# A fused RWKV-6 and FP4 feed-forward kernel: third down product among the levels, decay exponentials and tree ahead of the rounding, W and K mixed on four row groups

## The reference

```
xn = layernorm(x)
# attention: 4 heads of 64
dxa = shift(xn) - xn;  xm = xn + dxa * miu_x
lora_h = tanh(xm @ A_lora)                        # 5 groups of 32
miu_f = lambda_f + lora_h_f @ B_lora_f            # f = w, k, v, r, g
x_f = xn + dxa * miu_f
k, v, r = x_k @ Wk.T, x_v @ Wv.T, x_r @ Wr.T;  g = silu(x_g @ Wg.T)
w = td_miu + tanh(x_w @ td_A) @ td_B
S_t = diag(exp(-exp(w_t))) S_(t-1) + k_t^T v_t;   y_t = r_t @ (S_(t-1) + u * k_t^T v_t)
att = (group_norm(y) * gamma + beta) * g @ Wo.T
# feed-forward, every operand of a product rounded to FP4 in blocks of 16
h = silu(q(xn) @ q(w_gate).T) * (q(xn) @ q(w_up).T)     # 704 hidden
out = x + att + q(h) @ q(w_down).T
```

## Time and profile before

| | us |
|---|---|
| median of 3 runs (lowest to highest) | 773.11 (772.06 to 779.34) |
| the profiled execution, its own time | 776.1 |
| span of its instructions | 774.3 |
| TensorE busy | 675.0 (87%) |
| VectorE busy | 633.1 (82%) |
| ScalarE / POOL busy | 286.8 / 335.4 |
| granted TensorE clock, mean | 0.97 |

### The profile page before, as it was taken

The page is one execution under the profiler, slowest core; times in us unless marked ns, Lnnn a source line. Parts: engine busy times, 40 slices in busy tenths (PEclk is TensorE's granted clock), DMA queues, the critical chain, the costliest instruction groups (busy, mean ns, idle before and its releaser), DMA issues.

```text
span 774.3 us, 17212 instructions
## 1 busy us (share of the span) xinstructions
PE 675.0 (87%) x6873; PEld 487.6 (63%) x6873; DVE 633.1 (82%) x1093; ACT 286.8 (37%) x500; POOL 335.4 (43%) x245
## 2 busy tenths in 40 slices
PE   1386779899999999899999999989999999999986
PEld 0143667567857677567857577567756587566764
DVE  1899877789877997799877998789888898879773
ACT  2033053532525244432525336342625335252321
POOL 2465344534472354534463254533454244622540
PEclk9869699999999999999999999999999999999999
DMA  6000000000000000000000100000000000000000
GB/s 216 36 0 27 3 2 2 1 28 3 29 0 1 29 30 1 1 27 3 29 1 1 28 3 28 1 28 2 30 0 1 28 3 29 1 0 2 30 1 27
DMA packets 13986, 13.70 MB, mean 18 GB/s; under 512 B 1889, under 2 KB 13665, under 8 KB 13921
## 3 DMA queue, kind: packets, MB, share of 16 engines
q1 hardware_dynamic: 13920, 12.73, 5.1%
HBM read 8.53 MB, written 4.19 MB: 16 GB/s over the span
## 4 chain that ended last, share of the span: by engine, by line
PE 41%; DVE 29%; issue 17%; ACT 5%; POOL 5%; SPq 2%; DMA 1%; DVEq 0%; POOLq 0%; ACTq 0%
PE ft L373 7%; PE gu L348 5%; DVE xx L989 5%; PE pair L548 4%; POOL kk L1315 4%; PE pair L440 4%; PE pair L334 3%; PE pair L489 3%; PE pair L323 3%; DVE att L1077 2%; PE pair L457 2%; DVE hv L1005 2%; PE pair L410 2%; DVE att L1075 2%; DVE hv L905 2%
## 5 line engine op out<-in xcount | busy, mean ns | idle before, releaser
L1288 POOL TENSOR_TENSOR xx<-xx,xnt 128x1024 f32<-128x1024 f32 x32 | 71.7, 2240 | 73.8 <-DVE xx L989 73.7
L373 PE MATMUL ft<-wdn,raw 128*128 128x256 f32 (+1 forms) x384 | 97.8, 397 | 3.5 <-ACT raw L730 3.5
L1297 POOL TENSOR_TENSOR raw<-hv,hsc 128x352 f32<-128x352 f32 x64 | 50.7, 792 | 112.5 <-DVE hv L907 112.5
L348 PE MATMUL gu<-wgu_hi,xqt_hi 128*128 128x352 f32 x256 | 89.9, 351 | 9.0 <-DVE hv L1005 9.0
L1315 POOL TENSOR_TENSOR kk<-kk,dt 128x512 f32<-128x512 f32 x48 | 58.9, 1227 | 86.8 <-PE pair L410 75.9
L334 PE MATMUL pair<-xx,wproj 128*128 128x512 f32 x192 | 90.4, 615 | 3.7 <-POOL xx L1288 3.0
L709 ACT ACTIVATE sg<-gu 128x352 f32<-128x352 f32 x64 | 29.7, 463 | 157.5 <-PE gu L348 157.4
L373 PEld LDWEIGHTS ft<-wdn,raw 128*128 128x128 f32 (+1 forms) x384 | 69.4, 192 | 26.2 <-issue 14.0
L348 PE MATMUL gu<-wgu_lo,xqt_hi 128*128 128x352 f32 x256 | 82.9, 324 | 0.0
L348 PE MATMUL gu<-wgu_hi,xqt_lo 128*128 128x352 f32 x256 | 82.8, 323 | 0.0
L410 PE MATMUL pair<-rr,kk 64*64 64x64 f32 (+1 forms) x2880 | 70.0, 230 | 12.3 <-DVE ee L1180 8.0
(11 more groups left out here) (145 smaller groups left out, 1347.3 us busy)
## 6 DMA issues: line engine op xcount, KB each, us to landing
xl<-in_x SPq DMA_DIRECT2D x8, 512.0 KB, 3.7
out<-raw SPq DMA_DIRECT2D x8, 512.0 KB, 2.8
raw<-in_w_gu SPq DMA_DIRECT2D x1, 1408.0 KB, 9.7
wproj<-in_w_proj SPq DMA_DIRECT2D x1, 1280.0 KB, 6.6
raw<-in_w_dn SPq DMA_DIRECT2D x1, 704.0 KB, 10.1
wblora<-in_b_lora SPq DMA_DIRECT2D x8, 32.0 KB, 1.8
walora<-in_w_lora SPq DMA_DIRECT2D x1, 160.0 KB, 3.1
wtdb<-in_td_b SPq DMA_DIRECT2D x2, 64.0 KB, 2.2
```

The costliest lines, as they stand in the source:

```text
L348: mm = pe.matmul(gu[:, part * 512:part * 512 + HI], xs[:, k, b * L:(b + 1) * L], ws[:, k, c0:c0 + HI], start=(n == 0), stop=(n == len(term ...
L373: mm = pe.matmul(dn, hxt[0:w, t, :], wdn[0:w, t, :], start=(t == 0), stop=(t == KT - 1))
L1288: pool.tensor_tensor(x3, x3, xnt0, ALU.add).then_inc(s_xx, 1)
L1297: pool.tensor_tensor(blocked(to), hidden_blocks(u), bcast(hsc[:, u % 2, 0, :], BLOCK), ALU.mult).then_inc(s_hx, 1)
```

## The change

- `MIX_AT` gives w and k a second place for their second half: tile 2 of `lh`, row groups 2 and 3. ScalarE fills it with a second tanh of 64 partitions; two further 32 KB loads fill B_lora there.
- `keep_busy` is gone. Down product 2 of the step before leaves the front and is cut in two: tiles 0 and 1 behind level 2, tiles 2 to 5 behind level 3. Its add stands in VectorE's levels, behind round 1, and goes to `ot` after the attention is added (as does the fourth); `add_attention` waits for two adds and not three.
- Level 4 comes ahead of gate/up 2; HT 3 moves behind level 5, ahead of gate/up 3; level 6 ahead of down product 3. ScalarE's `hidden` 3 moves from the front's end to between keeps 5 and 6.
- VectorE's levels: `head_stats` stands ahead of product 2; scale 2 ahead of rescale 6.
- ScalarE does the decay exponentials and the affine ahead of `head_abs`; VectorE the tree ahead of `gated`, and `head_round` behind `ffn_product` 6 (step 0 keeps its own place for it). POOL adds R's xn ahead of `head_scale`.
- The query transposes and the high copy go behind G's projection and its SiLU.
- In `finish` the output projection goes ahead of HT 3, and `add_attention` ahead of the third add.

```diff
-MIX_AT = {W_MIX: [(0, 0), (0, 0)], K_MIX: [(0, 1), (0, 1)], ...
+MIX_AT = {W_MIX: [(0, 0), (2, 2)], K_MIX: [(0, 1), (2, 3)], ...
+            for f, g in ((W_MIX, 2), (K_MIX, 3)):
+                sp.dma_start(wblora[R_LORA * g:R_LORA * (g + 1), 2, :], b_lora[f]).then_inc(s_const, 16)
...
-            def keep_busy(step, n):
-
-                pe.wait_ge(s_hxt, before(step, 4))
-                for _ in range(n):
-                    pe.matmul(ft[:, 0:N], wgu_hi[:, 0, 0:P], xqt_hi[:, 0, :], start=True, stop=True)
...
+            def down_tiles(step, b, tiles):
+                if tiles[0] == 0:
+                    pe.wait_ge(s_hxt, before(step, 4) + b + 1)
+                for t in tiles:
                     w = P if t < KT - 1 else REST
                     mm = pe.matmul(dn, hxt[0:w, t, :], wdn[0:w, t, :], start=(t == 0), stop=(t == KT - 1))
-                mm.then_inc(s_dn, 1)
+                    if t == KT - 1:
+                        mm.then_inc(s_dn, 1)
@@ TensorE, front @@
                     y_transposes(prev)
-                    down(prev, 2)
                     gate_up(prev, 6)
...
                 project(pair[1], 2, R_MIX).then_inc(s_rmm, 1)
-                head_transposes_q(step)
                 pe.wait_ge(s_mix, before(step, 5) + 5)
                 pe.wait_ge(s_xx, before(step, 5) + 5)
                 project(pair[0], 3, G_MIX).then_inc(s_gmm, 1)
+                head_transposes_q(step)
@@ TensorE, finish @@
                 down(step, 2)
+                output_projection(step)
                 hidden_transposes(step, 3)
-                output_projection(step)
                 down(step, 3)
@@ TensorE, levels @@
                 level(step, 1)
-                if tail:
-                    hidden_transposes(step - 1, 3)
                 gate_up(step, 0)
                 level(step, 2)
                 if tail:
-                    keep_busy(step, 3)
+                    down_tiles(step - 1, 2, range(0, 2))
                 gate_up(step, 1)
                 level(step, 3)
                 if tail:
-                    keep_busy(step, 3)
+                    down_tiles(step - 1, 2, range(2, KT))
+                level(step, 4)
                 gate_up(step, 2)
-                level(step, 4)
-                if tail:
-                    keep_busy(step, 3)
+                level(step, 5)
+                if tail:
+                    hidden_transposes(step - 1, 3)
                 gate_up(step, 3)
-                level(step, 5)
+                level(step, 6)
                 if tail:
                     down(step - 1, 3)
-                level(step, 6)
@@ ScalarE, front @@
-                act.activation(lh[:], both(pair[0][:]), ACT.Tanh).then_inc(s_lh, 1)
+                act.activation(lh[:, 0:2], both(pair[0][:]), ACT.Tanh).then_inc(act_own, act_did.one())
+                act.activation(lh[HS:P, 2], pair[0][0:HS, 0:N], ACT.Tanh).then_inc(s_lh, 1)
...
-                head_abs(step)
                 act.wait_ge(s_wmm, through(step))
...
                     affine(prev)
+                    head_abs(step)
                     silu(prev, 6)
...
-                head_xqt(step)
...
                 act.activation(gg[:], both(pair[0][:]), ACT.Silu).then_inc(s_g, 1)
-                if tail:
-                    hidden(prev, 3)
+                head_xqt(step)
@@ ScalarE, levels @@
                 silu(step, 1)
-                silu(step, 2)
                 hidden_abs(step, 1)
                 keep_block(step, 4)
+                silu(step, 2)
+                keep_block(step, 5)
+                if tail:
+                    hidden(step - 1, 3)
                 silu(step, 3)
-                keep_block(step, 5)
                 keep_block(step, 6)
@@ VectorE, front @@
-                head_round(step)
-                if tail:
+                    head_round(step)
+                if tail:
+                    decay_tree(step)
                     gated(prev)
-                    add_down(prev, 2)
                 stream(step, R_MIX, 3, pair[1])
...
                     ffn_product(prev, 6)
-                    decay_tree(step)
+                    head_round(step)
                     add_attention(prev)
                     ffn_scale(prev, 6)
@@ VectorE, levels @@
                 keep_level(step, 3)
-                ffn_product(step, 2)
                 rescale_queries(step, 4)
                 ffn_round(step, 1)
+                if tail:
+                    add_down(step - 1, 2)
                 if more:
                     head_stats(step + 1)
+                ffn_product(step, 2)
+                rescale_queries(step, 5)
+                ffn_scale(step, 2)
+                rescale_queries(step, 6)
                 ffn_product(step, 3)
-                rescale_queries(step, 5)
                 if tail:
                     add_down(step - 1, 3)
-                rescale_queries(step, 6)
-                ffn_scale(step, 2)
                 ffn_scale(step, 3)
```

More of the change, by code:

```diff
@@ L52 @@
 LORA_AT = [[W_MIX, K_MIX, V_MIX, R_MIX], [G_MIX, G_MIX, R_MIX, V_MIX]]
-MIX_AT = {W_MIX: [(0, 0), (0, 0)], K_MIX: [(0, 1), (0, 1)], V_MIX: [(0, 2), (1, 3)], R_MIX: [(0, 3), (1, 2)], G_MIX: [(1, 0), (1, 1)]}
+MIX_AT = {W_MIX: [(0, 0), (2, 2)], K_MIX: [(0, 1), (2, 3)], V_MIX: [(0, 2), (1, 3)], R_MIX: [(0, 3), (1, 2)], G_MIX: [(1, 0), (1, 1)]}
 LN_EPS = 1e-5
@@ L127, in build @@
         walora = sb("walora", [P, HALVES, 2 * P])
-        wblora = sb("wblora", [P, 2, C])
+        wblora = sb("wblora", [P, 3, C])
         wtda = sb("wtda", [P, HALVES, TD_R])
@@ L153, in build @@
         xmt = sb("xmt", [P, HALVES, N])
-        lh = sb("lh", [P, 2, N])
+        lh = sb("lh", [P, 3, N])
         xx = sb("xx", [P, MIXES, HALVES, N])
@@ L224, in build @@
         out_v = out.rearrange("b (c t) k -> c t b k", t=L)
-        CONST_LOADS = 18
+        CONST_LOADS = 20
         weight_groups = []
@@ L367, in hidden_transposes, with down @@
                 tr.then_inc(s_trh, 1)
-            def down(step, b):
-                pe.wait_ge(s_hxt, before(step, 4) + b + 1)
-                for t in range(KT):
+            def down_tiles(step, b, tiles):
+                if tiles[0] == 0:
+                    pe.wait_ge(s_hxt, before(step, 4) + b + 1)
+                for t in tiles:
                     w = P if t < KT - 1 else REST
                     mm = pe.matmul(dn, hxt[0:w, t, :], wdn[0:w, t, :], start=(t == 0), stop=(t == KT - 1))
-                mm.then_inc(s_dn, 1)
+                    if t == KT - 1:
+                        mm.then_inc(s_dn, 1)
+            def down(step, b):
+                down_tiles(step, b, range(KT))
             def level(step, n):
@@ L606, in levels @@
                 if tail:
-                    keep_busy(step, 3)
+                    down_tiles(step - 1, 2, range(2, KT))
+                level(step, 4)
                 gate_up(step, 2)
-                level(step, 4)
-                if tail:
-                    keep_busy(step, 3)
-                gate_up(step, 3)
                 level(step, 5)
                 if tail:
+                    hidden_transposes(step - 1, 3)
+                gate_up(step, 3)
+                level(step, 6)
+                if tail:
                     down(step - 1, 3)
-                level(step, 6)
                 if not tail:
@@ L1030, in add_down @@
                 v.wait_ge(s_res, through(step))
-                to = fo if b < B - 1 else ot
-                if b == B - 1:
+                to = fo if b < 2 else ot
+                if b >= 2:
                     v.wait_ge(s_att, through(step))
@@ L1105, in add_attention @@
                 v.wait_ge(s_omm, through(step))
-                v.wait_ge(s_fo, before(step, 4) + 3)
+                v.wait_ge(s_fo, before(step, 4) + 2)
                 if later(step):
@@ L1195, in finish @@
                 gated(step)
+                add_attention(step)
                 add_down(step, 2)
-                add_attention(step)
                 add_down(step, 3)
@@ L1294, in scale_hidden @@
                 elif u % 2 == 0 and later(step):
-                    pool.wait_ge(s_trh, before(step, 4))
+                    pool.wait_ge(s_trh, before(step, 4) + u // 2 - 1)
                 to = hx[:, (u // 2) % 2, (u % 2) * HI:(u % 2 + 1) * HI]
@@ L1347, in front @@
                     scale_weights(3)
+                add_x(step, R_MIX, 3)
                 head_scale(step)
-                add_x(step, R_MIX, 3)
                 add_x(step, G_MIX, 4)
```

## The result

The change takes 781.07 us in the median of 20 runs, beside 777.06 for the kernel before, measured with it: a ratio of 1.0053 (95% interval 1.0037 to 1.0070). It is half a per cent slower. One slow run of each kernel, 928.5 us (mean granted clock 0.68) and 975.4, is left out of the ratio. The prediction was 766.3, 0.9% faster, with a range up to 779.

What follows compares the result with a forecast made beforehand. The prediction took TensorE to bound the front and VectorE the levels. Seven steps -7.7, start +0.9, last step -2.0 and end +2.0 gave -6.8 us: 769.3 from the profiled execution, 766.3 off the median, range 757 to 779.

Steps and rivals of the forecast that it cites:

- W and K on four groups: Front: four row groups run side by side, so W and K cost one mix, 0.85 us less a step.
- Wait before gate/up 3: Levels: gate/up 3 waits for product 2, now behind the next step's statistics; TensorE idles 2.05 us.
- The last step: Without next statistics, product 2 comes 2.3 us earlier: -2.0 us, beside the -1.1 of every step.
- rival 2: Steps: without fillers the clock falls to half twice a step, 12 dips more, +20 us, 787; chance 0.05.
- The steps' own gain: Front gains 2.6 us, levels give back 2.3, row groups save 0.85: each step 1.1 shorter, 86.8 for 87.9.
- The end's order: Finish: with the output projection first, the last transposes, copy and down product lose their cover: +2.0 us.
- The start: Two more 32 KB loads in SP's queue, awaited by TensorE's first transposes: +0.9 us, ends 0 to 0.93.
- The starting point: Profiled execution, 776.1 us, lies 3.0 over the median of the runs shown, 773.11; so 769.3 became 766.3.
- Rival 1: Front's gain is eaten ahead of level 1, levels still cost 2.3: +1.5 us a step, +10, 783.5; chance 0.1.
- Rival 3: W/K mix: row groups don't overlap, +0.85 us in each of seven steps, 772.3; chance 0.17.
- Rival 4: VectorE loses less to POOL, or the fourth gate/up isn't kept waiting: step gains 2.2 us, 758.6; chance 0.22.
- Rival 5: Steps: the change only moves work, each gain met by a wait, -0.2 us a step, 773; chance 0.06.

Runs made afterwards that it cites:

- run 1: The kernel before with only the second halves of the w and k mix on row groups 2 and 3, their second tanh and two loads: 775.4 us, 0.9974.
- run 10: The kernel before with the row groups alone, as in run 1, and three more fillers behind gate/up 6: 771.09 us, 0.9946.
- run 2: The changed kernel with the next step's statistics behind product 2 and rescale 5 on VectorE, in place of ahead of them: 756.99 us, 0.9766.
- run 3: The changed kernel with seven filler products, result unread, between hidden transposes 3 and gate/up 3: 775.64 us, 0.9990.
- run 4: The changed kernel with the finish in the order of before (hidden transposes 3 ahead of the output projection, third add ahead of the attention's): 776.44 us, 1.0004.
- run 9: The changed kernel with fillers in both TensorE gaps, seven products before gate/up 3 and three behind gate/up 6: 774.02 us, 0.9971.
- run 5: The changed kernel with the edits of run 2 and run 4, and B_lora in six loads in place of ten: 751.00 us, 0.9679.
- run 7: The kernel of run 2 with only the tree back behind ffn_product 6, ahead of head_round: 764.01 us, 0.9838.
- run 6: The kernel of run 2 with the front's order of before for the decay on ScalarE, VectorE and POOL: 788.60 us, 1.0156.

## Why the prediction was wrong

**The mechanisms of the steps were right.** W and K on four groups: 0.85 us forecast, 1.14 for 1.99 us in the trace, 0.8 a step in runs 1 and 10 (steps 2 to 7). Tree: 2.4 forecast, 2.38 measured. R's mix behind the exponential with 0.8 idle: 0.94. Output projection behind R's stream, level 1 at 59.5 us behind the recurrence with 1.6 idle: 59.5 and 1.37. Wait before gate/up 3: 2.05 forecast, 1.97 measured, and run 2 shows that it and the row behind it cost 2.1 us a step. The last step, without statistics: -3.1 forecast, -3.4 measured.

**The clock is the step that failed.** The prediction kept the clock of the kernel before, two dips in the steps, 3.4 us of price, and gave a worse clock, as rival 2, a chance of 0.05, on a row of step 0's levels with 57% busy and full clock. That row was no evidence for the tail of the later levels, which now had a gap of 1.97 us and one of 0.61 around its row of work. Nor does it hold for its own place: the same window of the change has 0.87, and in each of the eleven other profiles a stretch of 3.4 us or more at half clock begins within step 0's levels, 93 to 110 us from the start.

```profile
100.00:110.00 10.00, 7.85 (x118) 7.07 (x119) 8.41 (x22) 4.03 (x9) 4.27 (x6) 0.87 0.01 2
```

The change has dips in the levels' tail of four steps. Step 1 takes 86.6 us without one (runs 3, 4 and 9), the next five 87.17, so they cost 1.4, 1.5, 3.1 and 3.1 us: 9.2 in all, 5.8 more than before. Run 9 takes them all away without touching the order. The end has 2.8 more: the last product, behind the two new gaps, ran mostly at half clock, 5.32 us for 2.95, and the transposes before it 1.36 for 0.85. That makes 8.6 us of the error. Rival 2 blamed the fillers' absence. Kernels 2 and 5 have no fillers either, and one dip each in steps 1 to 7; what they also lack is the wait of 1.97 us.

**The steps' own gain was mis-sized.** Without dips five steps gain 0.7 us each and step 1 gains 1.25, 4.7 in all, and not 6.6: by the trace, product 2 starts 79.05 us behind the recurrence where the walk had 78.9, gate/up 3 79.6 for 79.5, and the next recurrence, behind level 6 and the down product, 87.17 for 86.8. Small delays along the serial row, each in the same direction, 1.9 us.

**The end's order and the start were mis-sized.** The order in the finish costs 2.7 us (run 4), +2.0 forecast. **The start:** +0.9 forecast; the first transposes came 1.5 later (17.83 for 16.35), in the other runs with ten loads 0.8 to 1.4, and the rest is step 0.

Together: 8.6 for the clock, 1.9 for the steps, 0.7 for the end's order and 0.9 for the start, less 0.3 for the last step, is the 11.8 us between -6.8 and +5.0.

**The starting point was wrong by 3.0 us.** The profiled execution gave 769.3. The prediction took 3.0 off, because this execution lay that far over the median of three runs. In the 20 runs the median before is 777.06, and the execution of 776.1 lies under it. These 3.0 and the 11.8 are the 14.8 us between 766.3 and 781.07. With the clock as forecast, 8.6 us less, the change would have been faster, as forecast, by some 4 us and not by 6.8.

Rival 1 named the right place (gate/up 3 and the serial row behind it) with the wrong cause: the front's gain didn't die. Rival 3 is out by the mix row. Rival 4 said that a step could gain 2.2 if the fourth gate/up weren't kept waiting; run 2 is that kernel, and gains 2.8. The walk had shown the wait and priced it, and still the sum left the clock as it was, with no room in the range for dips behind the wait. Rival 5, 0.2 us a step, is too low for the 0.7 measured in steps without a dip.

What the page SBUF — State Buffer of the Trainium skill, section Who interferes with whom, says of VectorE and GpSimd held in both directions: the tree is 1.76 us shorter away from POOL, and `head_round`'s first part 1.77 longer next to it; run 7 turns both round again (3.86 and 1.22 us). The page TensorEngine Tiling (Array Packing) of the Trainium skill, section Theoretical Speedup, gives up to 4x; here four groups took 1.14 us where pairs took 1.99, a factor of 1.75 on two.

## What to carry to other kernels

Behind an engine that must wait, look at what the engine it waits for has queued: two lines that put a 2.4 us job of VectorE behind the product that TensorE waited for took 24 us off, more than the whole change was after. Some 13 of them are the wait and the row behind it, and most of the rest is clock. When a change opens a new wait on an engine that is busy 85% of the time, price the wait and, as a rival with a chance worth naming, half clock behind it. Taking the fillers out didn't cost by itself here: kernels 2 and 5 have none, and fewer dips in their profiles than the kernel before. Fillers helped where they stood inside a wait, and cost 1.6 us in the last step, where there was none. A walk of one step can be right to 0.4 us and still miss the sign, if the clock of that step is taken from the kernel before.

## What the runs showed of the hardware

A dip in steps 1 to 7 began inside a TensorE gap or within 2.3 us of its end: the one ahead of R's mix (0.92 in before and run 1, 0.94 in runs 2, 3, 5 and 7), 1.9 to 1.97 ahead of gate/up 3 (the change, run 4), 3.91 in run 6, where every step had one; one more in run 6 stood behind gaps of 1.47 and 0.74 us at the end of step 0. But the length of a gap alone doesn't tell: the 1.3 to 1.4 us ahead of level 1 drew none in 63 steps of nine profiles, though longer than the 0.94. What else it takes no run isolates. With the gap before gate/up 3 filled there were no dips behind it, but run 3's profile had three behind the other gap; with both filled there were none. One profile of each kernel can't tell whether they moved or came by chance. In the longest execution of run 1 a gap as long as before drew one in six steps of seven where before had two; the step was only 0.8 us shorter. Why a given step is hit and the next is not stays open. At half clock 3.4 us of work that paces the kernel cost 1.4 to 1.7, and 6.8 us cost 3.1; the two dips of run 7, in the front, cost 0.1 us or less (86.47 for 86.41).
